# Attention and a quantised linear layer on one core: where o is divided by its key sums

## The reference

```python
x = x + attn(layernorm(x))        # 16 heads of 32 features, softmax over 2048 keys
x = x + ffn(layernorm(x))         # one 512 x 512 linear layer

# attn
scores = q @ k.T / sqrt(32) + band        # band: 0.1 where |i - j| <= 2
out = softmax(scores) @ v                 # per head
return out @ Wo.T + bo

# ffn: activations and weights rounded to an FP6 (E2M3) grid in blocks of 32
xd, wd = mx_quantize(x), mx_quantize(weight)
return xd @ wd.T + bias
```

## Time and profile before

| | us |
|---|---|
| median of three runs (lowest to highest) | 4577.78 (4577.1 to 4581.52) |
| profiled execution, its own time | 4576.01 |
| its span, first to last instruction | 4574.1 |
| project, from the start | about 650 |
| attend, about | 650 to 4126 |
| finish | 4126 to 4574 |

### The profile page before, as it was taken

One profiled execution on the slowest core, in us unless ns is written; L12 is line 12 of the kernel. 1 busy time (PEld: TensorE's weight loads), 2 busy tenths in 40 slices (PEclk: granted clock), 3 DMA queues, 4 the chain that ended last, 5 costly groups with the idle time before them and its releaser, 6 DMA issues. The chain is left out here.

```text
span 4574.1 us, 62800 instructions
## 1 busy us (share of the span) xinstructions
PE 4436.7 (97%) x22928; PEld 2504.6 (55%) x22928; DVE 3378.5 (74%) x5663; ACT 2446.5 (53%) x4652; POOL 2828.9 (62%) x927
## 2 busy tenths in 40 slices
PE   7999989999999999999999999999999999977999
PEld 6888845454445444444445454444454444525777
DVE  5444467888888888788787888888888788735776
ACT  2222216666666666666666666666666666651121
POOL 2111017778878787787877778878787787870000
PEclk9999969999999999999999999999999999988999
DMA  7666545555565656565656555565656565445452
GB/s 253 206 212 205 197 120 118 129 124 131 125 140 117 140 113 145 110 144 121 142 118 132 128 124 131 125 140 117 140 113 144 112 144 117 104 89 199 147 178 108
DMA packets 287700, 640.71 MB, mean 140 GB/s; under 512 B 40641, under 2 KB 107201, under 8 KB 249538
## 3 DMA queue, kind: packets, MB, share of 16 engines
q0 software_dynamic: 36864, 268.45, 29.3%
q1 hardware_dynamic: 250562, 368.66, 27.0%
HBM read 211.82 MB, written 156.24 MB: 80 GB/s over the span
## 5 line engine op out<-in xcount | busy, mean ns | idle before, releaser
L702 DVE TENSOR_REDUCE part_max<-ps_m 128x1 f32<-128x512 f32 x4096 | 2548.9, 683 | 654.0 <-PE ps_m L598 650.5
L772 POOL TENSOR_TENSOR pair<-p_sb 128x2048 f32<-128x2048 f32 x512 | 2348.4, 4587 | 665.5 <-ACT p_sb L690 301.9
L690 ACT ACTIVATE p_sb<-ps_s 128x512 f32<-128x512 f32 x4096 | 2114.8, 602 | 1130.3 <-PE ps_s L618 1129.8
L618 PE MATMUL ps_s<-q_st,k_st 97*128 97x512 f32 x4096 | 1732.4, 425 | 17.1 <-ACT p_sb L690 17.1
L598 PE MATMUL ps_m<-k_st,q_st 96*128 96x512 f32 x4096 | 1646.0, 405 | 42.0 <-POOL k_st L765 20.1
L618 PEld LDWEIGHTS ps_s<-q_st,k_st 97*128 97x128 f32 x4096 | 774.0, 189 | 1031.4 <-ACT p_sb L690 619.3
L632 PE MATMUL ps_o<-p_sb,v_sb 128*32 128x512 f32 x8192 | 1092.4, 605 | 0.2 <-DVE p_sb L729 0.2
L598 PEld LDWEIGHTS ps_m<-k_st,q_st 96*128 96x128 f32 x4096 | 785.7, 192 | 230.6 <-DVE part_max L702 76.3
L632 PEld LDWEIGHTS ps_o<-p_sb,v_sb 128*32 128x32 f32 x8192 | 161.3, 108 | 345.2 <-ACT p_sb L690 289.3
L166 POOL TENSOR_TENSOR xb<-xin,bo_row 128x2048 f32<-128x2048 f32 x16 | 75.3, 4706 | 424.7 <-DMA xin<-in_x 414.0
L642 PE MATMUL ps_d<-pair,ones 128*32 128x512 f32 x2048 | 267.5, 594 | 9.9 <-DMA pair<-pair 9.9
(11 more groups left out here) (94 smaller groups left out, 2678.4 us busy)
## 6 DMA issues: line engine op xcount, KB each, us to landing
pair<-pair POOLq DMA_DIRECT2D x256, 1024.0 KB, 7.3
q_st<-q_hi_d SPq DMA_DIRECT2D x128, 256.0 KB, 4.2
k_st<-k_hi_d SPq DMA_DIRECT2D x128, 256.0 KB, 5.5
xin<-in_x SPq DMA_DIRECT2D x16, 1024.0 KB, 8.2
xb_d<-xb SPq DMA_DIRECT2D x16, 1024.0 KB, 5.2
q_hi_d<-s_hi SPq DMA_DIRECT2D x64, 256.0 KB, 2.0
q_lo_d<-s_lo SPq DMA_DIRECT2D x64, 256.0 KB, 2.3
k_hi_d<-s_hi SPq DMA_DIRECT2D x64, 256.0 KB, 2.3
```

The costliest lines, as they stand in the source:

```text
L618: nc.tensor.matmul(ps_s[:, (HG * s + h) % RING_S, :], k_st[0:ROWS + 1, unit // QC % 2, kt // TT, h, kt % TT * P:(kt % TT + 1) * P], q_st[0 ...
L690: nc.scalar.activation(p_sb[:, s % SLOTS, h, :], ps_s[:, (HG * s + h) % RING_S, :], ACT.Exp, scale=SCALE).then_inc(p_ready, 1)
L702: nc.vector.tensor_reduce(part_max[:, unit % 2, col, n:n + 1], ps_m[:, seq % RING_M, :], AX.X, ALU.max).then_inc(max_taken, 1)
L772: nc.gpsimd.tensor_tensor(pair[:, m % PAIR_RING], p_sb[:, s % SLOTS], p_sb[:, (s + 1) % SLOTS], ALU.add).then_inc(paired, 1)
```

## The change

The scaling of o and its split into two parts leave `attend`. There ACT now copies o into a tile of its own, and SP stores it as it is (one store of 256 KB, at kt 4). The key sums are stored for each unit as before, but they are loaded, inverted and stored back once for the four units of a group (128 x 64 values; `load_den` at kt 9 and `store_rec` at kt 15 of the first unit after the group, `invert` at m = 6). For the last group this is done at the start of `finish`. `finish` loads for each chunk the raw o (one DMA of 1 MB) and the inverses (four DMAs of 256 KB, one for each head group, in the form of the former L536). POOL multiplies and subtracts (four and four instructions of 128 x 512 for a chunk), ACT makes the high parts; for chunk 0 DVE stands in for POOL.

```diff
@@ attend, sync @@
             def store_o(unit):
-                sp.wait_ge(o_split, unit + 1)
-                sp.dma_start(o_hi_d[unit], f32(o_hi[:])).then_inc(o_out, 16)
-                sp.dma_start(o_lo_d[unit], f32(o_lo[:])).then_inc(o_out, 16)
+                sp.wait_ge(o_copied, unit + 1)
+                sp.dma_start(o_d[unit], o_st[:]).then_inc(o_out, 16)
...
-            def load_rec(unit):
-                sp.wait_ge(rec_out, 16 * (unit + 1))
-                sp.dma_start(rec_b, rec_d[unit].unsqueeze(1).to_broadcast([HG, HD, CH])).then_inc(rec_loaded, 16)
+            def load_den(g):
+                sp.wait_ge(sum_out, 16 * QC * (g + 1))
+                sp.dma_start(den[:], keys_of(sum_d, g)).then_inc(den_loaded, 16)
...
@@ attend, scalar: o_high at kt 14 goes; copies wait for the stores of their own tile @@
-                at_least(act, o_out, 32 * unit)
-                nc.scalar.activation(sum_st, ps_d[:], ACT.Copy).then_inc(sum_copied, 1)
+                at_least(act, sum_out, 16 * unit)
+                nc.scalar.activation(sum_st[:], ps_d[:], ACT.Copy).then_inc(sum_copied, 1)
@@ attend, vector @@
-                if m % PAIRS == 4 and m > PAIRS:
-                    invert(m // PAIRS - 1)
+                if m % (QC * PAIRS) == 6 and m > PAIRS:
+                    invert(m // (QC * PAIRS) - 1)
@@ attend, gpsimd @@
-                if m % PAIRS == 5 and m > PAIRS:
-                    scale_o(m // PAIRS - 1)
-                if m % PAIRS == 6 and m > PAIRS:
-                    o_low(m // PAIRS - 1)
@@ finish, sync @@
             def load_o(c):
-                at_least(sp, out_projected, TT * (c - 1))
-                sp.dma_start(f32(o_hi[:, c % 2]), o_by_chunk(o_hi_d, c)).then_inc(o_in[c % 2], 16)
-                sp.dma_start(f32(o_lo[:, c % 2]), o_by_chunk(o_lo_d, c)).then_inc(o_in[c % 2], 16)
+                at_least(sp, o_split, NHG * (c - 1))
+                sp.dma_start(o_raw[:, c % 2], o_by_chunk[c]).then_inc(o_in[c % 2], 16)
+                if c == NCH - QC:
+                    sp.wait_ge(rec_last, 16)
+                for g in range(NHG):
+                    sp.dma_start(o_rec[:, c % 2, g, :],
+                                 rec_d[g * NCH + c].unsqueeze(1).to_broadcast([HG, HD, CH])).then_inc(rec_in[c % 2], 16)
...
+            load_o(0)
             sp.dma_start(f32(wo_hi[:]), wo_hi_d).then_inc(wo_in[0], 16)
-            load_o(0)
...
+            sp.dma_start(den[:], keys_of(sum_d, NG - 1)).then_inc(den_in, 16)
             load_o(1)
...
+            sp.wait_ge(den_turned, 1)
+            sp.dma_start(keys_of(rec_d, NG - 1), rec[:]).then_inc(rec_last, 16)
@@ finish, gpsimd @@
+            for c in range(1, NCH):
+                b = c % 2
+                if c == 1:
+                    pool.wait_ge(o_split, NHG)
+                pool.wait_ge(o_in[b], 16 * (c // 2 + 1))
+                pool.wait_ge(rec_in[b], 16 * NHG * (c // 2 + 1))
+                for g in range(NHG):
+                    nc.gpsimd.tensor_tensor(o_raw[:, b, g, :], o_raw[:, b, g, :], o_rec[:, b, g, :],
+                                            ALU.mult).then_inc(o_scaled, 1)
+                for g in range(NHG):
+                    pool.wait_ge(o_high, NHG * c + g + 1)
+                    nc.gpsimd.tensor_tensor(o_lo[:, b, g, :], o_raw[:, b, g, :], f32(o_hi[:, b, g, :]),
+                                            ALU.subtract).then_inc(o_split, 1)
@@ finish, scalar @@
+            def o_highs(c):
+                at_least(act, out_projected, TT * (c - 1))
+                for g in range(NHG):
+                    act.wait_ge(o_scaled, NHG * c + g + 1)
+                    nc.scalar.activation(o_hi[:, c % 2, g, :], o_raw[:, c % 2, g, :], ACT.Copy).then_inc(o_high, 1)
+
+            o_highs(0)
             act.wait_ge(consts2, 2)
             act.wait_ge(fb_in, 16)
             nc.scalar.activation(fb[0:1, :], fb_raw[:], ACT.Copy).then_inc(fb_split, 1)
+            o_highs(1)
             normalise(0)
             for c in range(NCH):
                 high(c)
                 if c + 1 < NCH:
                     normalise(c + 1)
+                if c + 2 < NCH:
+                    o_highs(c + 2)
@@ finish, vector: before the first residual, for chunk 0 @@
+            for g in range(NHG):
+                nc.vector.tensor_tensor(o_raw[:, 0, g, :], o_raw[:, 0, g, :], o_rec[:, 0, g, :],
+                                        ALU.mult).then_inc(o_scaled, 1)
+            for g in range(NHG):
+                v.wait_ge(o_high, g + 1)
+                nc.vector.tensor_tensor(o_lo[:, 0, g, :], o_raw[:, 0, g, :], f32(o_hi[:, 0, g, :]),
+                                        ALU.subtract).then_inc(o_split, 1)
+            v.wait_ge(den_in, 16)
+            nc.vector.reciprocal(rec[:], den[:]).then_inc(den_turned, 1)
@@ finish, tensor, in out_project @@
-                    if t == 0:
-                        pe.wait_ge(o_in[c % 2], 32 * (c // 2 + 1))
                     for k in range(NHG):
+                        if t == 0:
+                            pe.wait_ge(o_split, NHG * c + k + 1)
```

More of the change, by code:

```diff
@@ L32, with keys_of @@
 NB = D // QBLK
+NDEN = QC * HG * CH // P
 GRID = 64.0
+def keys_of(part_d, g):
+    return part_d[QC * g:QC * (g + 1)].rearrange("u h t -> (u h t)").rearrange("(p n) -> p n", p=P)
 def at_least(eng, sem, value):
@@ L74, in build @@
                 q_hi_d, q_lo_d, k_hi_d, k_lo_d, v_d, xb_d, wo_hi_d, wo_lo_d, wd_hi_d, wd_lo_d)
-        attend(nc, sem, ident, band_f, q_hi_d, q_lo_d, k_hi_d, k_lo_d, v_d, o_hi_d, o_lo_d, sum_d, rec_d)
-        finish(nc, sem, ident, ffn_b, xb_d, wo_hi_d, wo_lo_d, wd_hi_d, wd_lo_d, o_hi_d, o_lo_d, out_ch)
+        attend(nc, sem, ident, band_f, q_hi_d, q_lo_d, k_hi_d, k_lo_d, v_d, o_d, sum_d, rec_d)
+        finish(nc, sem, ident, ffn_b, xb_d, wo_hi_d, wo_lo_d, wd_hi_d, wd_lo_d, o_d, sum_d, rec_d, out_ch)
 def blocks(ap):
@@ L412, in _, with attend @@
                     products(c, n)
-def attend(nc, sem, ident, band_f, q_hi_d, q_lo_d, k_hi_d, k_lo_d, v_d, o_hi_d, o_lo_d, sum_d, rec_d):
+def attend(nc, sem, ident, band_f, q_hi_d, q_lo_d, k_hi_d, k_lo_d, v_d, o_d, sum_d, rec_d):
     NU = NG * QC
@@ L551, in _ @@
                             store_sum(unit - 1)
-                        if kt == 8:
-                            load_den(unit - 1)
-                        if kt == 10:
-                            store_rec(unit - 1)
-                        if kt == 11:
-                            load_rec(unit - 1)
+                        if kt == 4:
+                            store_o(unit - 1)
+                    if 0 < unit < NU and u == 0:
+                        if kt == 9:
+                            load_den(g - 1)
+                        if kt == KT - 1:
+                            store_rec(g - 1)
                     if unit == NU:
@@ L579, in _ @@
                         put_shift(unit + 1)
-                    if kt == KT - 1 and unit > 0:
-                        store_o(unit - 1)
-            store_o(NU - 1)
-            sp.wait_ge(o_out, 32 * NU)
+            sp.wait_ge(o_out, 16 * NU)
             sp.wait_ge(sum_out, 16 * NU)
-            sp.wait_ge(rec_out, 16 * NU)
+            sp.wait_ge(rec_out, 16 * (NG - 1))
         @block.tensor
@@ L682, in _ @@
                     copy_sum(unit - 1)
-                if kt == 14 and unit > 0:
-                    o_high(unit - 1)
                 if s >= SLOTS:
@@ L693, in _ @@
             copy_sum(NU - 1)
-            o_high(NU - 1)
         @block.vector
@@ L792, in finish @@
         [sem(f"xb_in{i}") for i in range(2)], sem("fb_in"))
+    rec_in = [sem(f"rec_in{i}") for i in range(2)]
+    o_scaled, o_high, o_split = sem("o_scaled"), sem("o_high"), sem("o_split")
+    den_in, den_turned, rec_last = sem("den_in"), sem("den_turned"), sem("rec_last")
     fb_split, fb_ready, consts2 = sem("fb_split"), sem("fb_ready"), sem("consts2")
```

53 lines of the change are left out of this document (17 added, 36 removed).

## The result

The kernel after takes 4630.07 us (median of five runs, 4625.66 to 4631.85), the kernel before 4578.74 us (five runs on the same chip): ratio 1.011, 95% interval 1.0096 to 1.0124. The forecast was 4601 with a range of 4552 to 4625, so the direction was right and the time lay 5 us above the range. The profiled execution of the kernel after has an own time of 4629.76 us and a span of 4628.0.

A forecast was written before the change was run, and what follows sets the result against it. PE was taken as the bound, busy in nearly all of attend and finish, so other engines' work counts only as PE stalls. 4576.0 - 28 (attend) - 14.5 (tail) + 15 (start) + 53 (loop) = 4601.5, said as 4601; range 4552 to 4625.

The forecast's parts named there:

- Attend, -28: Attend: work leaving POOL, ACT, DVE and SP removes PE stalls, 28 us saved, bounds 18 and 35.
- What PE felt is a collision: Attend: DVE's two-input SBUF product doesn't run during a POOL product; band product 1.77 us against 0.16, so PE waits.
- The tail, -14.5: Between attend and finish: the block ends once the sums have landed, so finish starts 14.5 us earlier, bounds -13.5 and -17.5.
- The start, +15: Start of finish: late inverses and POOL's products delay the first transpose by 15 us, bounds +3 and +20.
- every 1 MB load behind them waits for its share on these four: Start of finish: 1 MB loads queue behind inverse loads on four DMA engines; 13 units of 2.6 us, 36.5 us with latency.
- The loop, +53: Loop of finish: a 59.9 us path over two chunks exceeds PE's 52.3, +7.6 seven times, +53 us; bounds 0 and 75.
- POOL's 4.6 and DVE's 1.2: Loop of finish: POOL and DVE products take turns with y_q and xd, costing POOL 4.6 us and DVE 1.2.
- the stall itself moves y_q and xd against POOL's work: Loop of finish: argument for POOL and DVE hardly meeting, a rival at 4561 us, chance 0.13.
- The clock: Loop of finish: clock down after waits of several us, counted with inverses at 3 us each in the upper bound of 75.
- Rival 1: Finish: inverses land as fast as ordinary loads, loop keeps 26.14 us, start costs 3; 4536.5 us, chance 0.12.
- Rivals 2 and 3: Loop of finish: POOL and DVE hardly meet, +13, 4561 us, chance 0.13; or loop pays about half, +26, 4575, chance 0.15.
- Rival 4: Attend: stalls stay because POOL's earlier pair sums meet the band products; 4629 us, chance 0.07.

The follow-up runs named there:

- e5: Kernel after with inverses loaded by head, loads of o one chunk earlier, and ACT's normalise(0) and high parts reordered in finish: 4544.21 us.
- e7: Kernel after with two POOL products of 128x512 put back into attend, their result not used: 4637.49 us.
- e11: Kernel before with ACT's o_high moved from kt 14 to kt 15 and POOL's o_low from m = 6 to m = 7: 5141.52 us.
- e12: Kernel after, inverse loads reading 32 distinct rows of each of 4 arrays instead of repeated rows, still on four DMA engines: 4627.65 us.
- e8: Kernel after, inverse loads reading 128 distinct consecutive rows instead of repeated rows, which spread over all DMA engines: 4564.87 us.
- e6: Kernel after with ACT's normalise(0) ahead of o_highs(1) at the start of finish: 4625.82 us.
- e4: Kernel after without the loads of inverses in finish; POOL and DVE multiply by a tile of ones: 4553.99 us.
- e9: Kernel after without POOL's four multiplications a chunk in finish (chunks 1 to 15), loads of inverses kept: 4578.03 us.
- e2: Kernel after with the loads of o and inverses issued one chunk earlier, ahead of a store on SP: 4567.13 us.

## Why the prediction missed, step by step

- **What bounds the kernel.** Right: work put on POOL, ACT and DVE in finish cost only what PE waited for, and e5 has that work with a PE that never waits in the loop.
- **Attend, -28.** The size was nearly right: from the first exponential to that of the last step attend took 3425.0 us before and 3393.4 after, -31.6. The step that failed is "What PE felt is a collision" of a DVE and a POOL product. With the collisions put back (e7), attend is 3400.3 us, so they are worth 6.9. 21.7 us lay in the steps from kt 13, and they are ACT's wait for the scaling, ahead of the exponentials: those steps are short in e7 (collisions, no wait) and in e11 (collisions, the wait moved). The last 3.0 us were not separated. The sum came near without the right mechanism, since it rested on the lengths of these very steps, whatever made them long. The sentence named "ACT makes its exponentials late behind o_high" as one of two ways, and the argument then followed the other.
- **The tail, -14.5.** Right: from the last step's first exponential to the first DMA of finish 34.3 us before, 19.6 after, -14.7.
- **The start, +15 (measured +25.8).** That the four loads use the same four engines, and that loads of 1 MB queue behind them, was right (e12 against e8). The term mis-sized is "every 1 MB load behind them waits for its share on these four", priced at 2.6 us a load: the other twelve engines did not do their share at full speed either (the packet times stand in the last section). From the issue to POOL's first product of chunk 1 it took 46.1 us, not 36.5, which is 9.6 of the 10.8 us missing; 1.0 more is one small instruction of the norm, nmr, which took 1.20 us beside POOL's subtractions and takes 0.16 alone. The way it named, over `normalise(0)` behind the copies on ACT, was one of two that end within about 1 us of each other (e6); the other, PE's `out_project(1)` ahead of the transposes, it didn't name. Without those loads nothing of the 25.8 is left but 1.4 (e4).
- **The loop, +53 (measured +72.1).** The path was named right, and its sum is close: 62.4 us instead of 59.9. Term by term, from the rows of the loop above: load 4256.99 - 4237.08 = 19.9 (18.4 forecast); POOL to the end of its low parts 4268.27 - 4256.99 = 11.3 (10.2 + 4.6); the first tile 1.1 (0.7); the other tiles 4279.29 - 4269.40 = 9.9 (10.1); DVE and ACT to the next issue 4299.50 - 4279.29 = 20.2 (15.9). So the two terms of the collision were mis-sized against each other, POOL's 4.6 and DVE's 1.2, and the sum is close in part by luck. POOL loses only 1.3 us here, to the end of xd: y_q and xd begin 15.8 and 19.2 us after the issue in this loop, not 19.4 and 22.8, and y_q is over before POOL begins. The mis-sized term is DVE's loss, 1.2 forecast and 5.5 measured. Of the 5.5, y_q has 0.44, xd 1.1 and qs (0.71 for 0.18) 0.5, and 3.4 fall to instructions that the prediction did not price at all: small ones of the norm, 128 x 4, of which three take 1.15 to 1.26 us each while POOL multiplies. e9 shows that it is the multiplications: without them these 5.5 us are gone. All of it is lost to POOL's work for the other chunk, of which the prediction's path has nothing: "the stall itself moves y_q and xd against POOL's work" looked at two large instructions and one chunk. Two chunks together take 61.9 to 64.6 us; six such pairs are 62.2 us over their 6 x 52.3, 10.4 each where 7.6 was forecast, and the first period and the last long one add 1.7 and 8.3: 72.
- **The stalls' own price.** The clock was a bound of the forecast, and it weighs little. Within a gap of 6.37 us the granted clock falls to 0.5 (1.2 GHz), for 6.8 us, of which the last 3.0 meet PE's matmuls; they take 0.63 us instead of 0.39 and begin 0.43 us apart. But PE takes POOL's low parts as they come then, one in 1.24 us for three matmuls: the first tile is late by 0.4 us.
- **The rivals.** Rival 1 (39.5 us faster than before) didn't hold, and e8 shows that it wouldn't have even with all engines: 4565, not 4536.5. With the load of o earlier and ACT's order changed as well (e5) the loop is back at its old length; which of the two e8 lacked was not tried apart. Rivals 2 and 3 fell since the loop paid its whole price (72.1 us, not 13 or 26). Rival 4 named nearly the right time, 4629, for a wrong reason: attend did lose its stalls, 31.6 us. The range was too narrow: the bounds of start and loop (+20, +75) by themselves reached to 4628.5, and the upper end was put at 4625.

The path could be opened at one place that the prediction passed over: that SP issues the loads of a chunk behind a store was taken as given in its sum, and it was worth 62 us (e2).

## What to carry to other kernels

When a side task moves into another stage, draw its path as a ring, from the release of a buffer to its next release, and price on it every instruction of each engine, also those that take 0.16 us alone: beside POOL's products each of them can cost as much as a whole instruction of POOL. Before sizing the loads, look at their leading dimension: the same bytes on four engines or on sixteen were 63 us apart here. And ask of each load what it waits for and what merely stands ahead of it in the issue order; of 72 us lost in the loop 62 came back by issuing the load before a store.

## What the runs showed of the hardware

- **Loads on four engines slow the packets of other loads too.** Beside loads on four engines, packets of 8 KB took 490 ns in 4091 to 4103 and 2 KB packets 136 ns (means over the packet records of the trace); in e8, where the loads are spread, they took 315 and 89 ns. The share was 1.00 at 259 GB/s against, in e8, this row:

```profile
4084.00:4103.00 19.00, 9.12 (x25) 6.80 (x26) 7.38 (x12) 3.07 (x5) 0.00 (x0) 0.56 1.04 403
```

  It doesn't hang on the repeated rows (e12: 516 ns, 250 GB/s). The trace doesn't name the engine of a packet, but the times of the packets of 2 KB add up to 3.7 engines over these 12 us and those of 8 KB to 12.0: an estimate by which the 8 KB packets ran on the engines that have no share in the loads of inverses. Why these slow down stays open.
- **SP stands in the issue.** Four issues of such loads took 19.47 us (4092.75), one of them 10.0; alone an issue takes about 0.6. Everything behind them on SP was late with them: the load of wd_hi was issued at 4112.26.
- **A scalar operation is blocked too.** DVE's TENSOR_SCALAR of 128 x 4 took 1.22 us beside POOL, 0.17 without. The Trainium skill (SBUF — State Buffer, "Who interferes with whom") names tensor_scalar among the operations that can take the shared port pair with one input; the row agrees, and the prediction had used only its rule for two inputs.
